# Gated cross attention and a mixture of experts: Q's low halves and K0b moved forward in the attention loop, three waits left out, 71 expert tiles instead of 72

## What is computed

```python
# x: 16 x 224 x 512, ctx: 16 x 750 x 512, 16 heads of 32
def attention(q_x, ctx, energy_coeffs):
    Q = heads(q_x @ Wq + bq); K = heads(ctx @ Wk + bk); V = heads(ctx @ Wv + bv)
    scores = einsum("bhqd,bhkd->bhqk", Q, K) / sqrt(32)
    energy = abs(energy_coeffs).mean(-1); energy = energy / (energy.max(-1) + 1e-8)
    scores = scores * ((energy > 0.1) * 0.9 + 0.1)        # one gate per key
    return (softmax(scores) @ V) @ Wo + bo

def ffn(flat):                                            # 3584 tokens
    out = sum over 2 shared experts of (silu(flat @ wg) * (flat @ wu)) @ wd
    weights, indices = top_k(softmax(flat @ router_w), 2) # of 16 routed experts
    out += sum over the 2 picked experts of weight * (silu(flat @ wg_e) * (flat @ wu_e)) @ wd_e
    return out

x = x + tanh(g_xattn) * attention(layernorm(x), ctx_1024, ctxb)
x = x + tanh(g_ffn)   * ffn(layernorm(x))
```

## Time and profile before

| | |
|---|---|
| median of 3 runs | 2041.23 us (2032.24 to 2041.59) |
| profiled execution | 2022.37 us |
| its span, first to last instruction | 2020.6 us |
| granted TensorE clock, mean | 0.983 |
| PE busy | 1928.0 us, 95% |
| DVE, ACT, POOL busy | 1111.3 us (55%), 787.1 us (39%), 1228.3 us (61%) |

### The profile page before, as it was taken

The page is one execution under the profiler, slowest core; times in us unless marked ns, Lnnn a source line. Parts: engine busy times, 40 slices in busy tenths (PEclk is TensorE's granted clock), DMA queues, the critical chain, the costliest instruction groups (busy, mean ns, idle before and its releaser), DMA issues. The chain is left out here.

```text
span 2020.6 us, 40620 instructions
## 1 busy us (share of the span) xinstructions
PE 1928.0 (95%) x12484; PEld 1497.8 (74%) x12485; DVE 1111.3 (55%) x1768; ACT 787.1 (39%) x1559; POOL 1228.3 (61%) x1385
## 2 busy tenths in 40 slices
PE   6799999999999999999999999999789989999999
PEld 5587877778787787878778787877567856666787
DVE  4565565656556565555656565564536723333477
ACT  3344454444545444454544444454442212222100
POOL 2377677777767677776777768676541533333473
PEclk9899999999999999999999999999799989999999
DMA  6754838365483836648374664837127164444796
GB/s 219 198 143 124 235 96 224 113 178 158 126 241 89 222 114 177 166 120 249 88 214 119 172 174 114 248 92 220 58 69 274 48 225 145 146 148 145 209 267 211
DMA packets 171498, 332.35 MB, mean 164 GB/s; under 512 B 20326, under 2 KB 69478, under 8 KB 170806
## 3 DMA queue, kind: packets, MB, share of 16 engines
q1 hardware_dynamic: 154460, 286.05, 49.6%
q0 software_dynamic: 10880, 33.56, 6.0%
q10 hardware_dynamic: 6112, 12.13, 1.7%
HBM read 215.09 MB, written 116.06 MB: 164 GB/s over the span
## 5 line engine op out<-in xcount | busy, mean ns | idle before, releaser
L940 DVE TENSOR_REDUCE neg_max<-score 112x1 f32<-112x750 f32 x512 | 480.4, 938 | 575.4 <-PE score L1247 574.4
L646 ACT ACTIVATE probs_t<-st 125x448 f32<-125x448 f32 x768 | 414.0, 542 | 514.0 <-PE st L1273 509.2
L515 POOL TENSOR_TENSOR acc<-acc,probs_t 125x448 f32<-125x448 f32 x256 | 310.4, 1212 | 74.6 <-ACT probs_t L646 73.4
L1273 PE MATMUL st<-q_stack,k_stack 98*125 98x224 f32 x1536 | 329.6, 297 | 1.8 <-ACT probs_t L646 1.3
L1211 PE MATMUL proj<-ctx_hi,weights 128*128 128x376 f32 (+1 forms) x1024 | 328.9, 346 | 0.0
L517 POOL TENSOR_TENSOR acc<-acc,probs_t 125x448 f32<-125x448 f32 x256 | 294.8, 1152 | 20.1
L1273 PEld LDWEIGHTS st<-q_stack,k_stack 98*125 98x125 f32 x1536 | 265.7, 188 | 53.5 <-issue 23.7
L1247 PE MATMUL score<-k_stack,q_stack 96*112 96x512 f32 (+1 forms) x1024 | 283.7, 358 | 20.3 <-DMA k_stack<-k_parts 12.5
L1221 PE MATMUL proj<-weights,ctx_hi 128*125 128x512 f32 x768 | 248.7, 405 | 4.8 <-issue 4.8
L507 POOL TENSOR_TENSOR acc<-probs_t 125x448 f32<-125x448 f32 x128 | 145.7, 1140 | 169.7 <-PE pv L1327 152.0
L1247 PEld LDWEIGHTS score<-k_stack,q_stack 96*112 96x112 f32 x1024 | 159.6, 178 | 75.2 <-issue 51.9
(11 more groups left out here) (238 smaller groups left out, 2761.6 us busy)
## 6 DMA issues: line engine op xcount, KB each, us to landing
k_stack<-k_parts SPq DMA_DIRECT2D x192, 375.0 KB, 6.3
ctx_raw<-in_ctx_t SPq DMA_DIRECT2D x64, 375.0 KB, 10.1
k_parts<-k_hi SPq DMA_DIRECT2D x64, 375.0 KB, 6.7
k_parts<-k_lo SPq DMA_DIRECT2D x64, 375.0 KB, 7.2
y_slots<-y_sb SPq DMA_DIRECT2D x72, 256.0 KB, 2.9
q_stack<-q_parts SPq DMA_DIRECT2D x64, 224.0 KB, 6.1
gu_sb<-in_w_gu ACTq DMA_DIRECT2D x4, 2048.0 KB, 15.3
x_in<-in_x SPq DMA_DIRECT2D x16, 448.0 KB, 9.2
```

The lines of the kernel that those rows point to most:

```text
L515: nc.gpsimd.tensor_tensor(both, both, tiles(c, p, pair, 0), ALU.add).then_inc(half_added, 1)
L646: act.activation(probs_t[0:KW, (c * PHASES + p) % 2, u % HC, :], st[u % 2][0:KW, 0:2 * L], ACT.Exp)\
L940: nc.vector.tensor_reduce(neg_max[:, h // HC % 2, h % HC, t:t + 1], score[0:QW, 0:S], axis=AX.X, op=ALU.max, negate=True).then_inc(maxed, 1)
L1273: ins = nc.tensor.matmul(st[u % 2][0:KW, k * L:(k + 1) * L], k_stack[0:SHIFTED, h, kt * KW:(kt + 1) * KW], q_stack[0:SHIFTED, h, :], start ...
```

## The change

Attention: on DVE, Q0's low half moves from behind the shift's low part to directly behind K0a's gate, and K0b's gate from behind to ahead of maximum (13, 0); on ACT, K0b's high copy moves from tick 10 to tick 8, behind `place_shift`; on POOL, K0b's low part moves ahead of an `add_pair`; on PE, `attend` no longer waits for V's copies. Routed experts: 7168 picks and up to 127 rows of padding for each of 16 experts need 71 tiles at most, so the last step has three tiles, and its third splits two chunks of columns.

```diff
@@ POOL, batch
                 if not last:
                     key_low(n, "K0a")
+                if not last:
+                    key_low(n, "K0b")
                 add_pair(b, 1, 2, 0)
-                if not last:
-                    key_low(n, "K0b")
@@ ACT, batch, chunk 1
                     if u == 8:
                         place_shift(b, 2, b)
+                        if not last:
+                            key_high(n, "K0b", b)
                     if not first and u in (8, 9):
...
-                    if not last and u == 10:
-                        key_high(n, "K0b", b)
@@ DVE, batch
                 next_maximum(b, 12, 0)
                 if not last:
                     gate_keys(n, "K0a", b)
+                    query_low(n, 0, b)
...
                 next_maximum(b, 12, 1)
...
                 shift_low(b, 2, b)
                 if not last:
-                    query_low(n, 0, b)
+                    gate_keys(n, "K0b", b)
                 next_maximum(b, 13, 0)
-                if not last:
-                    gate_keys(n, "K0b", b)
-                else:
+                if last:
                     shared_low(3)
@@ PE, attend
-                if c == 0:
-                    body = b if p == 2 else -1 if fixed and b == 0 else b - 1
-                    for kt in (2 * p, 2 * p + 1):
-                        pe.wait_ge(proj_read[bank_of(body, f"V{kt}")], turn_of(body, f"V{kt}") + 1)
@@ experts
+USED_TILES = (TOP * T + E_R * (P - 1)) // P
...
-    y_slots = nc.dram_tensor("y_slots", (SLOT_TILES * P, D), F32, kind="Internal").ap()
+    y_slots = nc.dram_tensor("y_slots", (USED_TILES * P, D), F32, kind="Internal").ap()
@@ routed_experts; POOL, SP, ACT and PE alike
+        LAST_TILES = USED_TILES - (STEPS - 1) * ASTEP
...
-                for k in range(ASTEP):
+                for k in range(tiles):
...
-            with pool.Fori(1, STEPS) as i:
-                step(i)
+            with pool.Fori(1, STEPS - 1) as i:
+                step(i, ASTEP)
+            step(STEPS - 1, LAST_TILES)
@@ routed_experts, DVE, last step
-                        split_columns(nc, dve, xc, xc_parts, first_high, k * DC // ASTEP, xc_ready,
-                                      range(k * DC // ASTEP, (k + 1) * DC // ASTEP))
+                        split_columns(nc, dve, xc, xc_parts, first_high, k, xc_ready,
+                                      range(k, k + 1 if k < tiles - 1 else DC))
```

More of the change, by code:

```diff
@@ L547, in batch @@
                     key_low(n, "K0a")
-                add_pair(b, 1, 2, 0)
                 if not last:
                     key_low(n, "K0b")
+                add_pair(b, 1, 2, 0)
                 add_pair(b, 1, 2, 1)
@@ L2268, in routed_experts @@
         STEPS = SLOT_TILES // ASTEP
+        LAST_TILES = USED_TILES - (STEPS - 1) * ASTEP
+        assert 2 < LAST_TILES <= ASTEP
         xg_t = sb("xg_t", [P, 2, DC, P])
@@ L2307, in take_waits, with step @@
                 nc.gpsimd.tensor_tensor(spare[:, n:n + 1], spare[:, 7:8], spare[:, 7:8], ALU.add).then_inc(spare_set, 1)
-            def step(i):
+            def step(i, tiles):
                 for k in range(ASTEP):
@@ L2322, in step @@
                         .then_inc(gathered[k], 16)
-            with pool.Fori(1, STEPS) as i:
-                step(i)
+            with pool.Fori(1, STEPS - 1) as i:
+                step(i, ASTEP)
+            step(STEPS - 1, LAST_TILES)
         @block.sync
         def _(sp):
-            def step(i):
-                for k in range(ASTEP):
+            def step(i, tiles):
+                for k in range(tiles):
                     sp.wait_ge(y_copied, i * ASTEP + k + 1)
                     sp.dma_start(y_slots[bass.ds((i * ASTEP + k) * P, P), :], y_sb[:, k, :]).then_inc(y_stored[k], 16)
-            step(0)
+            step(0, ASTEP)
             load_columns(sp, xc, xn_cols, HEAD, xc_in)
-            with sp.Fori(1, STEPS) as i:
-                step(i)
+            with sp.Fori(1, STEPS - 1) as i:
+                step(i, ASTEP)
+            step(STEPS - 1, LAST_TILES)
         @block.scalar
@@ L2349, in step @@
             def step(i, first, last):
-                for k in range(ASTEP):
+                for k in range(LAST_TILES if last else ASTEP):
                     q = i * ASTEP + k
@@ L2360, in step @@
                 if last:
-                    copy_y(SLOT_TILES - 1, ASTEP - 1, i, False)
+                    copy_y(USED_TILES - 1, LAST_TILES - 1, i, False)
             step(0, True, False)
@@ L2386, in step @@
             def step(i, first, last):
-                for k in range(ASTEP):
+                tiles = LAST_TILES if last else ASTEP
+                for k in range(tiles):
                     q = i * ASTEP + k
@@ L2390, in step @@
                         copy_h(q - 1, (k - 1) % 2, first and k < 3)
-                    if not (last and k == ASTEP - 1):
+                    if not (last and k == tiles - 1):
                         copy_x(q + 1, k + 1, first and k < 1)
@@ L2399, in step @@
                         dve.wait_ge(xc_in, 16 * BATCHES)
-                        split_columns(nc, dve, xc, xc_parts, first_high, k * DC // ASTEP, xc_ready,
-                                      range(k * DC // ASTEP, (k + 1) * DC // ASTEP))
+                        split_columns(nc, dve, xc, xc_parts, first_high, k, xc_ready,
+                                      range(k, k + 1 if k < tiles - 1 else DC))
             copy_x(0, 0, True)
             loop(dve, step)
-            copy_h(SLOT_TILES - 1, ASTEP - 1, False)
+            copy_h(USED_TILES - 1, LAST_TILES - 1, False)
         @block.tensor
@@ L2458, in step @@
                     gate_up(q, k, expert, (2, 3))
-                    after = expert_of(tile_expert, q + 1) if k < ASTEP - 1 else None
-                    if k < ASTEP - 1:
+                    after = expert_of(tile_expert, q + 1) if k < tiles - 1 else None
+                    if k < tiles - 1:
                         turn(q + 1, k + 1, i, first and k == 0)
@@ L2467, in step @@
                 if last:
-                    turn_hidden(SLOT_TILES - 1, ASTEP - 1, False)
-                    down(SLOT_TILES - 1, ASTEP - 1, before, False)
+                    turn_hidden(USED_TILES - 1, LAST_TILES - 1, False)
+                    down(USED_TILES - 1, LAST_TILES - 1, before, False)
             turn(0, 0, 0, True)
@@ L2580, in _ @@
             for k in range(ASTEP):
-                pool.wait_ge(y_stored[k], 16 * (SLOT_TILES // ASTEP))
+                pool.wait_ge(y_stored[k], 16 * ((USED_TILES - 1 - k) // ASTEP + 1))
             take_waits(5)
```

## The result

The changed kernel takes **2014.47 us** in the median of 4 runs (2012.53 to 2016.87), beside 2040.6 us of the kernel before in 4 (2032.24 to 2041.59): a ratio of 0.9886, 95% interval [0.9865, 0.9906]. The forecast was 2015.0. The agreement is closer than the working deserves, and in part luck: one term was 3 us too large, and nearly as much that no part explains makes up for it.

A forecast was written before the change was run, and what follows sets the result against it. PE was taken to set the pace in the attention loop, busy 1314.74 of 1341.50 us. Terms 12.8 + 9.6 + 1.4 + 2.4 = 26.2 us, off the 2041.23 median, gave 2015.0 us; range 2003 to 2028.

The forecast's parts named there:

- Part 1, Q's low half: Attention loop: Q1's first product no longer waits for Q0's low half; 15 x 0.86, less 0.1, gains 12.8 us.
- Part 2, K0b's three steps: Attention loop: K0's parts complete 3.1 us sooner, shortening the next batch's first score's wait for K's stack; gains 9.6 us.
- the K stack can follow at 648.4, when K's parts have landed too: 2.4 us sooner: SP queue, turn 6: K-stack loads issued at 648.4 instead of 650.81, against a need of 2.0 us.
- a DMA share of 0.19: DMA engines between 641 and 646 us: taken as slack for the earlier load, against 0.98 between 651 and 659.
- the prediction's own signs: First K-stack load issued about 8.3 us after Q1's start (9.85 before); no score wait on it left in the loop.
- the third rival: Landings scatter, about half of the stack's waits stay: 21.4 us gained, 2019.8; counted with the forecast, together 0.80.
- the rule that was weighed and set aside there: Issuers share 16 DMA engines, so issuing sooner gives no bandwidth; alone it meant the landing-not-sooner rival's intermediate case, 2022.4 us.
- ACT's order and POOL's adds at nothing: Attention loop: K0b's copy delays ACT's exponential to about 643.5, cover 1.2 us; POOL's sum 0.6 us sooner; no cost.
- the second rival: ACT's K0b copy waits for DVE's gate, delaying an exponential and PE's score column; 4 us late gives 2057; chance 0.03.
- Part 3, V: PE's product with V in attention: dropping the waits for V's copies saves 0.1 x 14 turns, 1.4 us.
- Part 4, 71 tiles: End of the routed experts: one tile fewer, 3.41 us, less 0.96 for a second split chunk; gains 2.4 us.

The follow-up runs named there:

- e9: Changed kernel, Q's DRAM buffer laid out in 128 contiguous rows per store, chunk 1's K-stack load held until chunk 3's shift rows land: 1988.01 us, ratio 0.9848.
- e3: Kernel before with only Q0's low half moved on DVE: ratio 0.9974, 5.3 us.
- e4: Kernel before with only K0b's gate, high copy and low part moved, Q's low half where it was: ratio 1.0007.
- e1_before: The kernel before, unchanged, measured and profiled once more: ratio 0.9992; profiled execution 2039.12 us.
- e8: Attention phase of the kernel before with the 71 tiles of the change: ratio 0.9986, 2.9 us below the kernel before.
- e2: The changed kernel, unaltered, measured again on the same chip as three other runs: 2008.01 us, ratio 0.9874.
- e11: The changed kernel, unaltered, measured once more on another chip: 1996.37 us, ratio 0.9888.
- e5: Changed kernel with Q's DRAM buffer laid out so each store writes 128 contiguous rows, Q stack loaded in three transfers: 2031.0 us, ratio 0.9977.

## Why the prediction was right, and where it wasn't

**What bounds the kernel: right.** PE sets the pace in the loop; every microsecond won was idle time of PE, and e9's turns, alike to 0.03 us, show what a turn is once the waits that scatter are gone. Q1's wait was 0.86 us by starts, as the prediction counted it, and not the 0.70 of the row.

**Part 1, Q's low half: right.** 1.03 us became 0.18, in every turn of the loop, and the half ends 1.2 us ahead of PE as forecast (at −1.02, PE at 0.18). What the prediction understated is that these 12.8 us are only kept if part 2 works too: alone (e3) they brought 5.3.

**Part 2, K0b's three steps: the step that was mis-sized.** The parts being complete 3.1 us sooner was right (3.17). The step that failed is "the K stack can follow at 648.4, when K's parts have landed too: 2.4 us sooner". It measured 1.4 (10.68 to 9.28), because K's stores landed 5.5 us after their issue where before it was 4.0. The prediction assumed that a store issued sooner lands sooner by as much, and read a DMA share of 0.19 as room. It was Q's stores filling four engines. Q's own landing moved less than it was taken to as well: the Q stack was forecast 2.0 us sooner and went out 1.1 sooner (medians 8.87 and 7.80), although Q's stores did begin 2.0 sooner; why they took longer no run shows. With 1.4 us instead of 2.4 against a need of 2.0 in turn 6, waits had to stay, and 7 of 14 did, 3.9 us. So two of the prediction's own signs failed: the first K-stack load is issued 9.1 us after Q1's start in the median, not about 8.3, and waits of the score on it are left. The loop's 14 turns won 19.9 us (1231.5 to 1211.6). Less 14/15 of 12.8 and the 1.4 of part 3 that leaves 6.5 for part 2, by subtraction, for 9.6; the wait's own rows, counted as the prediction counts them, give 10.1 less 5.0, 5.1 us. That is near the third rival in its size, though not by its reason: the landings are late by 1 us on the whole, not scattered. Taking the whole 2.4 us, with nothing off for the transfers ahead, was the choice that went wrong; the rule that was weighed and set aside there, that issuers share the DMA engines (the Trainium skill, DMA: Bandwidth & Descriptors, section "Issuing engines are not separate DMA queues"), was nearer to what the runs show than the row's mean of 0.19.

The two parts are worth much more together than apart: e3 won 5.3 us and e4 nothing (−1.4), while the whole change won 19.9 in the loop, of which 1.4 are part 3. K's landing comes after the later of two things, its own stores' issue and Q's stores' end. In the kernel before both stand at the same place (10.7), so moving one alone moves K's landing by next to nothing (10.84 in e3, 10.73 in e4).

**ACT's order and POOL's adds at nothing: right.** No wait of `st` on `probs_t` was added in the loop (one, 1.3 us, as in e1_before), which rules out the second rival. ACT's copy starts at 634.49, right behind the two DMA issues (633.08 + 1.30), while the gate has ended at 633.71, so it never stood waiting for DVE.

**Part 3, V: right in size.** In turn 6 the product in chunk 0 starts 0.30 us behind the score column instead of 0.42:

```profile
608.47 0.38 PE L1272 MATMUL st<-q_stack,k_stack 98*125 98x224 f32 x2
608.77 0.96 PE L1286 MATMUL pv<-probs_t,v_sb 125*32 125x224 f32 x16
```

Counted from the column's last product, the mean over the 14 turns went from 289 to 199 ns in the first third and from 458 to 446 in the second, 1.4 us in all, as forecast. No run took this part alone, so that the turn gains it is argued, not shown.

**Part 4, 71 tiles: right.** From the second tile to the last stage 254.5 us became 251.7, 2.7 us, and e8 says 2.9 [0.4, 5.5] by its interval. The last tile's two chunks of columns now fill 1861.65 to 1863.42, 1.77 us where one took 0.96, so the second cost 0.81:

```profile
1861.65 0.69 DVE L2241 CAST xc_parts<-xc 128x448 fp32r<-128x448 f32 x2
1862.26 1.16 DVE L2244 TENSOR_TENSOR xc_parts<-xc,xc_parts 128x448 fp32r<-128x448 f32 x2
```

**The sum.** 12.8 + 6.5 + 1.4 + 2.7 = 23.4 us for 26.2. The medians differ by 26.1 us in the first comparison, 28.6 on the chip of e2 and 22.6 on that of e11, so the 23.4 lie at the lower edge; up to 5 us remain that the parts don't account for and that runs of different chips don't agree on. That 26.1 meets the forecast's 26.2 is luck to that extent: what part 2 fell short by, 3.1 us, is made up by 2.7 that nothing here explains.

## What to carry to other kernels

Before a transfer is costed by its issue, look at the DMA share around it together with the rate: a share near a quarter while one kind of store runs was stores on four engines here, and what was issued behind them on all sixteen landed 1.5 us later for it (5.5 us after its issue instead of 4.0). Where two chains meet at a wait, price each part alone by the later one; sums of separately priced parts hold only when all are made. And when a whole queue moves forward, list the small transfers that someone waits for and ask which big one now goes out ahead of them; an explicit hold on the big one can be worth more than its speed (e5 to e9: from 0.9977 to 0.9848 of the kernel before, each on its own chip).

## What was not expected of the hardware

- Two transfers of 3.5 KB, issued 1.6 us behind one of 1125 KB, came so late that PE stood for up to 2.3 us a turn (e5); issued ahead of it they cost nothing (e9).
- A stall of PE put down to issue, 5.4 to 13.8 us, with the clock down to 0.50 within it, in nine profiles, and none in four: the first of the kernel before and the three of e9 to e11. Programs that are the same stand on both sides. Its cause is open.
- On one chip the kernel before measures 17 us (0.8%) below what it does on two others, the changed kernel 12 below e2; the changed kernel's ratio to the kernel before stayed within 0.9874 to 0.9888.
